# A decoder layer on one core: the experts' gates on the input rows, biases as contraction rows, a two-part second product summed in PSUM

## The reference

```python
scores = jnp.einsum('bsd,de->bse', x, Wr) + br
_, topk_idx = jax.lax.top_k(scores, K)
indicator = jax.nn.one_hot(topk_idx, E, dtype=scores.dtype).sum(-2)
weights = jax.nn.softmax(jnp.where(indicator > 0, scores, neg_inf), axis=-1)
for i in range(E):
    xi = x * indicator[..., i:i + 1]
    h = jax.nn.relu(jnp.einsum('bsd,dh->bsh', xi, W1[i]) + b1[i])
    yi = jnp.einsum('bsh,hd->bsd', h, W2[i]) + b2[i]
    out = out + yi * weights[..., i:i + 1]
```

## Time and profile before

| | |
|---|---|
| time, median of 3 runs | 346.68 us (345.67 to 348.85) |
| span of the profiled execution, first to last instruction | 345.2 us, 5907 instructions |
| median less the span | 1.5 us |
| VectorE busy | 205.2 us (59%) |
| ScalarE busy | 166.1 us (48%) |
| GpSimd busy | 56.2 us (16%) |
| mean granted TensorE clock | 0.975 of 2.4 GHz |
| cross attention of b = 3, its first score to the first `H` | 214.6 to 231.5 us |
| experts, first `H` to the end | 231.5 to 345.2 us |

### The profile page before, as it was taken

How to read it: one execution, slowest core, us unless ns; L and a number is a source line. 1 busy time by engine, 2 the same in 40 slices (tenths; PEclk the granted TensorE clock), 3 DMA queues, 4 the chain that set the end, 5 groups by cost and what they waited for, 6 DMA issues and landing times.

```text
span 345.2 us, 5907 instructions
## 1 busy us (share of the span) xinstructions
PE 311.9 (90%) x2177; PEld 233.1 (68%) x2194; DVE 205.2 (59%) x470; ACT 166.1 (48%) x482; POOL 56.2 (16%) x88
## 2 busy tenths in 40 slices
PE   6468999999998989797978888889999999999995
PEld 2356767787786667455634433458889998899895
DVE  3979766555639684974487886245455444433432
ACT  2435976747845664366445677844122112211310
POOL 5730047031003200740110201120020000000000
PEclk9859999999999999999989998999999999999999
DMA  7800002551100010001003680000000000100001
GB/s 220 202 1 1 2 2 38 65 63 18 41 6 3 4 46 0 0 5 47 2 5 66 237 235 3 2 0 2 0 2 1 3 0 2 30 2 0 2 0 30
DMA packets 13868, 11.98 MB, mean 35 GB/s; under 512 B 2600, under 2 KB 10896, under 8 KB 13840
## 3 DMA queue, kind: packets, MB, share of 16 engines
q1 hardware_dynamic: 13840, 11.61, 14.3%
HBM read 7.84 MB, written 0.52 MB: 24 GB/s over the span
## 4 chain that ended last, share of the span: by engine, by line
PE 74%; DVE 18%; issue 3%; ACT 3%; DMA 1%; another core or an unknown queue 0%; DVEq 0%; ACTq 0%
PE ps L775 17%; PE ps L514 7%; PE ps L515 7%; PE ps L516 7%; PE ps L587 6%; PE ps L620 4%; PE ps L632 4%; DVE mneg L1127 4%; PE ps L665 4%; PE ps L701 4%; PE ps L686 2%; PE ps L594 2%; PE ps L622 2%; DVE negmax L1096 2%; DVE norm L1010 2%
## 5 line engine op out<-in xcount | busy, mean ns | idle before, releaser
L891 ACT ACTIVATE p<-ps,negmax 128x256 f32<-128x256 f32 (+1 forms) x128 | 52.8, 431 | 25.5 <-DVE negmax L1096 25.2
L775 PEld LDWEIGHTS ps<-w_raw,hid 128*128 128x128 f32 x512 | 59.5, 192 | 1.4
L775 PE MATMUL ps<-w_raw,hid 128*128 128x128 f32 x512 | 59.6, 275 | 0.0
L943 ACT ACTIVATE hid<-ps,b1T 128x512 f32<-128x512 f32 x32 | 21.9, 688 | 73.8 <-PE ps L516 73.8
L1127 DVE TENSOR_REDUCE mneg<-ps 128x2 f32<-128x512 f32 x64 | 42.3, 684 | 14.3 <-PE ps L665 13.5
L920 ACT ACTIVATE px<-ps 128x512 f32<-128x512 f32 x64 | 35.4, 602 | 18.9 <-PE ps L686 15.9
L1219 DVE SCALAR_TENSOR_TENSOR resid<-ps,wgt,resid 128x128 f32<-128x128 f32 x64 | 18.0, 345 | 42.8 <-PE ps L775 42.8
L1096 DVE TENSOR_REDUCE negmax<-ps 128x2 f32<-128x512 f32 (+1 forms) x48 | 32.9, 686 | 17.3 <-PE ps L589 11.0
L665 PE MATMUL ps<-k_st,q_mem 128*128 128x256 bf16 x128 | 24.9, 278 | 8.9 <-DVE mneg L1127 8.1
L1200 DVE TENSOR_SCALAR hid<-ps,b1T 128x512 f32<-128x512 f32 x32 | 23.8, 749 | 10.9 <-PE ps L516 10.8
L877 ACT CAST t_hi<-ps 128x512 fp32r<-128x512 f32 x32 | 18.7, 594 | 20.9 <-PE ps L516 20.4
(11 more groups left out here) (175 smaller groups left out, 555.8 us busy)
## 6 DMA issues: line engine op xcount, KB each, us to landing
w_raw<-in_L_ffn_W SPq DMA_DIRECT2D x1, 2048.0 KB, 9.3
w_in<-in_L_attn_W_qkv SPq DMA_DIRECT2D x4, 384.0 KB, 5.2
k_st<-k_part SPq DMA_DIRECT2D x12, 128.0 KB
q_mem<-q_part SPq DMA_DIRECT2D x48, 32.0 KB
resid<-in_x SPq DMA_DIRECT2D x1, 512.0 KB, 4.6
p<-in_L_attn_W_o SPq DMA_DIRECT2D x1, 512.0 KB, 6.6
p<-in_ctx SPq DMA_DIRECT2D x1, 512.0 KB, 7.8
out_dram<-resid SPq DMA_DIRECT2D x2, 256.0 KB, 2.3
```

What stands on the lines that cost most here:

```text
L775: last = pe.matmul(ps[:, Y_BANK[k % 2], P * tt:P * tt + P], hid[:, k % 2, c, P * tt:P * tt + P], w2_sb[:, NC * e + c, :], start=(c == 0), ...
L891: last = act.activation(dst, bank[:, n * i:n * i + n], ACT.Exp, bias=negmax[:, kt, h:h + 1], accum_out=psums[:, kt, h:h + 1])
```

## The change

Four things change together.

First, the gate moves from the output to the input. Since relu is positively homogeneous and gates are not negative, gate x expert(x) equals the expert applied to gate x x, if the biases are scaled with it. A new unit `X` for each pass spreads the expert's gates over 128 partitions with one matmul (`gate_rows`), VectorE multiplies them with the transposed rows `nT` into `x_f` (`gated`), ScalarE makes the high part `x_hi` (`gated_high`), and VectorE the low part `x_lo` (`gated_low`). `H` of pass k waits for `x_lo` of pass k.

Second, biases enter by a contraction row. Normed rows sum to zero over their 128 columns, so the last column is dropped for a column of ones, the last row of W1 is subtracted from the other 127, and b1 takes its place. W1 is hence loaded as 127 rows, b1 as the 128th, and the dropped row is loaded once more, spread over all partitions (`w1_last`). GpSimd does the subtraction in eight steps (`first_weights`), and `WS` on ScalarE waits for these. The router's weights get the same treatment. The bias b2 is one float32 matmul for each half, in the pass with `B2`.

Third, the second product is two-part too. It has 12 matmuls of 128 x 512 columns, adds up in one PSUM bank over all eight experts of a half, and comes out transposed; at the end of a half `YE` copies it and `YO` transposes and adds it to `resid`. W2 is cut into parts by new units `W2` (ScalarE, in the slots of b = 3) and `second_weights` (GpSimd). For it, all four quarters of `hid` get a high part on ScalarE (`relu_high`) and a low part on VectorE (`relu_low`).

Fourth, `RT`, `GT` and `WT` of the first half move up into the slots of b = 3, and the five steps `oq0` to `wo` of the last batch element, which stood between `H` units of passes 0 to 3, stand together ahead of the first `H`.

```diff
+LAST = D - 1
+LOW = 32
...
+        px, w1_last, _, w2_hi, g_lo, t_hi, t_lo = overlay(
+            [("px", 4096, F32), ("w1_last", 4096, F32)], [("px_too", 4096, F32), ("w2_hi", 4096, F32R)],
+            [("g_lo", 2048, F32R), ("t_hi", 3072, F32R), ("t_lo", 3072, F32R)])
...
-            more = {(2, 1): [("b1", 0)], (3, 1): [("NT", 0)], (3, 7): [("RT", 0)]}
+            more = {(3, 1): [("NT", 0)], (3, 2): [("RT", 0)], (3, 4): [("GT", 0)], (3, 7): [("WT", 0)]}
...
-                if b == 2:
-                    slot += [("WS", 0, g)]
+                if b >= 2:
+                    slot += [("WS" if b == 2 else "W2", 0, g)]
...
+        slots.append([("X", 0), ("oq0", last), ("oT0", last), ("oq1", last), ("oT1", last), ("wo", last)])
+        extra = {3: [("NT", 1)], 4: [("RT", 1)], 5: [("GT", 1)], 6: [("WT", 1)], 9: [("YO", 0, 0), ("YO", 0, 1)]}
         for k in range(2 * NE):
-            more = extra.get(k, []) + [None, None]
-            units = [("H", k, 0), more[0], ("H", k, 1), ("H", k, 2), more[1], ("H", k, 3)]
-            slots.append([u for u in units if u] + ([("Y", k - 1)] if k else []))
-        slots.append([("Y", 2 * NE - 1)])
...
+            units = [("YE", 0, 0), ("YE", 0, 1)] if k == NE + 1 else []
+            units += [("H", k, 0), ("H", k, 1)] + ([("X", k + 1)] if k + 1 < 2 * NE else [])
+            units += [("H", k, 2)] + extra.get(k, []) + [("H", k, 3)]
+            if k % NE == 2:
+                units += [("B2", k // NE)]
+            slots.append(units + ([("Y", k - 1)] if k else []))
+        slots.append([("Y", 2 * NE - 1), ("YE", 1, 0), ("YE", 1, 1), ("YO", 1, 0), ("YO", 1, 1)])
...
-            sp.dma_start(w1_raw[:, :].rearrange("p (e n) -> p e n", n=HID), w1.rearrange("e p n -> p e n")
-                         ).then_inc(s_w12[0], 16)
+            sp.dma_start(w1_raw[0:LAST, :].rearrange("p (e n) -> p e n", n=HID),
+                         w1[:, 0:LAST, :].rearrange("e p n -> p e n")).then_inc(s_w12[0], 16)
+            sp.dma_start(w1_raw[LAST:D, :], b1.rearrange("e n -> (e n)").unsqueeze(0)).then_inc(s_w12[0], 16)
+            sp.dma_start(w1_last[:, :].rearrange("p (e n) -> p e n", n=HID), w1[:, LAST, :].partition_broadcast(P)
+                         ).then_inc(s_wlast, 16)
+            sp.wait_ge(s_zero, 1)
+            for r in (0, LOW):
+                sp.dma_start(b2_sb[r:r + NE, :], b2).then_inc(s_b2, 16)
             stack_m(2)
-            sp.dma_start(w2_sb, w2.rearrange("e (c p) d -> p (e c) d", p=P)).then_inc(s_w12[1], 16)
+            sp.dma_start(w2_raw[:, :].rearrange("p (n d) -> p n d", d=D), w2.rearrange("e (c p) d -> p (e c) d", p=P)).then_inc(s_w12[1], 16)
...
             for hf in range(2):
...
-                sp.wait_ge(s_acc, NE * (hf + 1))
-                sp.dma_start(out.rearrange(tiles, p=P)[:, 4 * hf:4 * hf + 4, :],
-                             resid[:, 4 * hf:4 * hf + 4, :]).then_inc(s_out, 16)
...
+                for i in range(2):
+                    ts = slice(4 * hf + 2 * i, 4 * hf + 2 * i + 2)
+                    sp.wait_ge(s_misc_ev, misc_at[("YO", hf, i)] + 1)
+                    sp.dma_start(out.rearrange(tiles, p=P)[:, ts, :], resid[:, ts, :]).then_inc(s_out, 16)
...
+                pool.wait_ge(s_mv3, TPB * (b + 1))
+                step(pool.memset(norm[:, TPB * b:TPB * b + TPB, LAST:D], 1.0))
+                norm_batch(2, b, s_mv3, s_n3, LAST)
+
+            def first_weights(i):
+                if i == 0:
+                    pool.wait_ge(s_w12[0], 32)
+                    pool.wait_ge(s_wlast, 16)
+                cols = slice(512 * i, 512 * i + 512)
+                pool.tensor_tensor(w1_raw[0:LAST, cols], w1_raw[0:LAST, cols], w1_last[0:LAST, cols], ALU.subtract
+                                   ).then_inc(s_wdiff, 1)
+
+            def second_weights(i):
+                pool.wait_ge(s_w2hi, i + 1)
+                cols = slice(512 * i, 512 * i + 512)
+                pool.tensor_tensor(w2_lo[:, cols], w2_raw[:, cols], w2_hi[:, cols].bitcast(F32), ALU.subtract
+                                   ).then_inc(s_w2lo, 1)
...
+            pool.wait_ge(s_misc, misc_at[("PJ", B - 1)] + 1)
+            pool.memset(b2_sb[:, :], 0.0).then_inc(s_zero, 1)
...
+            pool.tensor_tensor(wr_sb[0:LAST, :], wr_sb[0:LAST, :], wr_last[0:LAST, :], ALU.subtract).then_inc(s_pick, 1)
+            for i in range(NE):
+                first_weights(i)
             norm_3(0)
             norm_3(1)
             norm_3(2)
+            for i in range(4):
+                second_weights(i)
             norm_3(3)
+            for i in range(4, NE):
+                second_weights(i)
...
+            def gate_rows(k):
+
+                e, hf = k % NE, k // NE
+                if k == 0:
+                    pe.wait_ge(s_pv_ev, 2 * B)
+                if e == 0:
+                    pe.wait_ge(s_misc_ev, misc_at[("WT", hf)] + 1)
+                ge(pe, s_xf, k)
+                pe.matmul(ps[:, X_BANK, :], pick[:, e, :], wgtT[:, 512 * hf:512 * hf + 512], start=True, stop=True
+                          ).then_inc(s_gt, 1)
...
+                e = k % NE
                 if k == 0 and c == 0:
                     pe.wait_ge(s_wlo, 8)
                     pe.wait_ge(s_px, 16 * B)
                     pe.wait_ge(s_mx_ev, 16 * B)
-                if k % NE == 0 and c == 0:
-                    pe.wait_ge(s_misc_ev, misc_at[("NT", hf)] + 1)
+                if c == 0:
+                    pe.wait_ge(s_xlo, k + 1)
                 if k >= 1:
-                    pe.wait_ge(s_ha if c % 2 == 0 else s_hd, 2 * (k - 1) + c // 2 + 1)
-                products(ps[:, H_BANK[c], :], [w[:, e, P * c:P * c + P] for w in w1_p], n_of(512 * hf, 512)).then_inc(s_h, 1)
+                    pe.wait_ge(s_hd, 4 * (k - 1) + c + 1)
+                products(ps[:, H_BANK[c], :], [w[:, e, P * c:P * c + P] for w in w1_p],
+                         [x[:, k % 2, :] for x in x_p]).then_inc(s_h, 1)
...
-                for tt in range(4):
-                    for c in range(NC):
-                        last = pe.matmul(ps[:, Y_BANK[k % 2], P * tt:P * tt + P], hid[:, k % 2, c, P * tt:P * tt + P],
-                                         w2_sb[:, NC * e + c, :], start=(c == 0), stop=(c == NC - 1))
...
+                e, hf = k % NE, k // NE
+                out_bank = ps[:, Y_BANK[hf], :]
+                pe.wait_ge(s_w2lo, e + 1)
+                for c in range(NC):
+                    pe.wait_ge(s_hd, 4 * k + c + 1)
+                    w, h = [w[:, NC * e + c, :] for w in w2_p], [x[:, k % 2, c, :] for x in hid]
+                    pe.matmul(out_bank, w[0], h[0], start=(e == 0 and c == 0), stop=False)
+                    pe.matmul(out_bank, w[1], h[0], start=False, stop=False)
+                    last = pe.matmul(out_bank, w[0], h[1], start=False, stop=(e == NE - 1 and c == NC - 1))
                 last.then_inc(s_y, 1)
+
+            def second_bias(hf):
+                pe.wait_ge(s_b2, 32)
+                pe.matmul(ps[:, Y_BANK[hf], :], b2_sb[:, :], wgtT[:, 512 * hf:512 * hf + 512].bitcast(F32),
+                          start=False, stop=False)
...
             def weight_high(i):
 
-                act.wait_ge(s_w12[0], 16)
+                act.wait_ge(s_wdiff, i + 1)
                 act.copy(w1_hi[:, 512 * i:512 * i + 512], w1_raw[:, 512 * i:512 * i + 512]).then_inc(s_whi, 1)
 
-            def relu(k, c):
+            def second_high(i):
+
+                act.wait_ge(s_w12[1], 16)
+                act.wait_ge(s_wdiff, NE)
+                act.copy(w2_hi[:, 512 * i:512 * i + 512], w2_raw[:, 512 * i:512 * i + 512]).then_inc(s_w2hi, 1)
+
+            def gated_high(k):
+                act.wait_ge(s_xf, k + 1)
+                act.wait_ge(s_px, 16 * B)
+                ge(act, s_h, 4 * (k - 1))
+                act.copy(x_p[0][:, k % 2, :], x_f[:, k % 2, :]).then_inc(s_xhi, 1)
+
+            def relu_high(k, c):
                 act.wait_ge(s_h, 4 * k + c + 1)
                 ge(act, s_y, k - 1)
-                act.activation(hid[:, k % 2, c, :], ps[:, H_BANK[c], :], ACT.Relu,
-                               bias=b1T[:, NC * (k % NE) + c:NC * (k % NE) + c + 1]).then_inc(s_ha, 1)
...
+            def gated(k):
+                hf = k // NE
+                dve.wait_ge(s_gt, k + 1)
+                ge(dve, s_xhi, k - 1)
+                dve.tensor_tensor(x_f[:, k % 2, :], ps[:, X_BANK, :], nT[:, 512 * hf:512 * hf + 512], ALU.mult
+                                  ).then_inc(s_xf, 1)
+
+            def gated_low(k):
+                dve.wait_ge(s_xhi, k + 1)
+                dve.tensor_tensor(x_p[1][:, k % 2, :], x_f[:, k % 2, :], x_p[0][:, k % 2, :].bitcast(F32), ALU.subtract
+                                  ).then_inc(s_xlo, 1)
+
+            def relu_low(k, c):
+                dve.wait_ge(s_ha, 4 * k + c + 1)
+                dve.scalar_tensor_tensor(hid[1][:, k % 2, c, :], ps[:, H_BANK[c], :], 0.0,
```

(1 more changed line is left out.)

230 lines of the change are left out of this document (118 added, 112 removed).

## The result

The changed kernel takes 453.86 us (median; 449.52 to 456.13), against 346.85 us (345.67 to 348.85) measured beside it: 1.307 times the time before, 95% interval 1.301 to 1.312. It is 107 us slower. The forecast was 433.5 us in a range of 418 to 455. The profiled execution took 449.52 us, with a span of 447.7.

A forecast was written before the change was run, and what follows sets the result against it. TensorE was taken to bound the kernel, busy 90% of the span. Span 345.2 + 81 (stall) + 2.5 (cross attention) + 3.3 (experts with entry) = 432.0, median 1.5 above: 433.5 us, range 418 to 455.

The forecast's parts named there:

- The cause: W1's load: 127 outer rows, a prime, go through one DMA engine at 25.4 GB/s, taking 81.8 us; chance 0.84.
- Case (2): W1's load is spread over the engines anyway, with a remainder: time 358.5 us; chance 0.10.
- case (3): W1's load goes through one slow engine at 8 GB/s and takes 260 us: 611 us; chance 0.03.
- The stall: TensorE's first score of b = 2 waits for `stack_m(2)` behind W1, from 198.06 to 279.3: 81 us later.
- Cross attention: Cross attention of b = 3: eight W2 casts on ScalarE with earlier `RT` and `WT` add 2.5 us, between 0 and 5.
- After a stall of 80 us TensorE may be granted less than full clock for a while: Cross attention behind the stall waits for VectorE and ScalarE anyway, so a lower TensorE clock was put at nothing.
- So it costs nothing beyond the 81: GpSimd's eight W1 subtractions, 1.1 us each, are covered by the stall, since ScalarE wants one every 2 us.
- the earlier `RT` and `WT`: First-half routing steps moved into cross attention of b = 3, counted within its 2.5 us.
- The way into the experts: From the last `CO` to the first `H`: a chain of 7.7 us in which TensorE hardly works.
- A pass: Each expert pass takes 6.1 us, set by VectorE's and ScalarE's chain, against TensorE's own 5.8 and 6.37 before.
- small steps of `YE`: Experts: an odd piece within 4.5 us that also holds `RT` and `GT` of the second half and b2 products.
- the engine's rate: Rate of the one engine carrying W1, 407 / 16 GB/s; 10% lower or higher is 8 us to either side.

The follow-up runs named there:

- b_127_1: The kernel before with only W1's load cut into 127 rows and one row, nothing else of the change: 425.96 us, 1.226 times the kernel before.
- f_nolast: W1's correction and `w1_last` load left out, against the changed kernel with 112 and 15 row loads and `w1_last` behind `stack_m(2)` (374.84 us): 368.12 us.
- f_exp: Gates' exponential at `GT` instead of `RT`, against the changed kernel with 112 and 15 row loads and `w1_last` behind `stack_m(2)` (374.84 us): 370.82 us.
- a_m2_first: The changed kernel with `stack_m(2)` issued ahead of W1 on SyncE's queue: 459.47 us, against 453.86 us for the changed kernel.
- a_122_5: The changed kernel with W1's 127 rows loaded as 122 rows and 5 rows: 414.10 us, against 453.86 us for the changed kernel.

## Why the prediction was right, and where its terms were off

**The cause was right.** One engine carries the 127 rows: share 0.07, 26 GB/s (predicted 0.06 and 25), and cutting the load differently moves the time to where the number of engines says. Case (2), a split with a remainder, is out; of case (3), 8 GB/s, nothing is seen. That the wait for `stack_m(2)` and that for the weights have one cause and don't add was right too: with the first taken away, the second stands for 92 us.

**The stall was put at 81 us and took 83.7.** TensorE began at 281.73, where 279.3 was expected. `w_last` was issued at 262.06 and landed 17.9 us later by the page, at 280.0, where I had 278.8; the copies of `stack_m(2)` came 1.8 us behind it, where I had 0.5. What I had wrong without a price is the queue: I had taken these copies to be waiting in it long since, but SyncE was held at the bias row (74.76 us) and at the two copies of `b2` (8.60 us) and issued them only from 271.16 to 275.25. That is still ahead of the landing of `w_last`, so no row shows that it cost anything.

**Cross attention was put at +2.5 us (0 to 5) and took +9.9.** This is the term that was off most, at twice its upper bound. The starts of `CO` show where. Here are the first and the third `CO` of b = 3 in the changed kernel, then in `b_127_1`, which has the same pause and none of the rest:

```profile
306.60 1.07 PE L758 MATMUL ps<-px,v_pad 128*32 128x256 f32 x16
...
320.38 1.94 PE L758 MATMUL ps<-px,v_pad 128*32 128x256 f32 x16
```

```profile
298.15 1.07 PE L702 MATMUL ps<-px,v_pad 128*32 128x256 f32 x16
...
306.04 1.07 PE L702 MATMUL ps<-px,v_pad 128*32 128x256 f32 x16
```

From the first score of b = 2 to the first of these it is 24.9 us in the changed kernel, 23.6 in `b_127_1` and 21.3 in the kernel before. So 2.3 us come with the pause ("After a stall of 80 us TensorE may be granted less than full clock for a while ... I put nothing for it"), and 1.3 with what the change adds to b = 2. There I had of GpSimd's eight subtractions "So it costs nothing beyond the 81". They took 1.33 us each where I expected 1.1. What was missed is VectorE, whose low parts of W1 beside them took 1.25 and 1.79 us in place of 0.68, and TensorE waits for maxima behind them (0.42, 1.17 and 0.54 us). The 4.0 us of `f_nolast` are not this price, since `w_last` came late there.

From the first to the third `CO` of b = 3 it is 13.8 us against 7.9, both in `b_127_1` and before: 5.9 us, the largest part. It is "the earlier `RT` and `WT`", with `GT`, which I had within the 2.5. `f_exp` brings the same stretch from 13.6 to 10.1, so in that base 3.5 us hang on the place of one exponential in ScalarE's order and on the clock behind it. W2's casts, the only part that I did count, stand here too; with six of them gone the stretch took 12.3, and the whole cross attention 0.7 less. The last 0.4 us lie behind the third `CO`. The shares of 2.3 and 1.3 come from one profiled execution each, and the clock dips at other places in each of them, so they are good to some tenths at best.

On VectorE beside GpSimd the rows come first: operations that read one input from PSUM didn't change (all 64 `hid_lo` 0.68 to 0.69, two maxima 1.28), and those with both in SBUF went from 0.68 to 1.79 at most; one `x_lo` beside GpSimd's work on W2, at 340.83, took only 0.73. The Trainium skill, "SBUF — State Buffer", section "SBUF: two separate sides", states that a VectorE operation with two SBUF inputs and a GpSimd operation that reads SBUF shut each other out for a whole instruction. This trace agrees in which operations suffer.

**The way into the experts was put at 7.7 us and took 9.1.** The chain was right; `x_lo` took 1.60 us in place of 0.68, beside GpSimd's low parts of W2, and TensorE's own pieces ran partly at half clock (0.78 on average).

**A pass was put at 6.1 us and took 6.15.** The chain of VectorE and ScalarE holds it, not TensorE's 5.8: at 416.56, as in other passes, TensorE's first weight load of a pass stands 0.52 us for `x_lo`. That load, and three starts of `x_f` in the changed kernel:

```profile
416.56 0.19 PEld L571 LDWEIGHTS ps<-x_hi,w_hi 128*128 128x128 f32 x1 [0.52 <-DVE x_lo L1301]
...
390.48 0.68 DVE L1296 TENSOR_TENSOR x_f<-ps,nT 128x512 f32<-128x512 f32 x1
...
396.64 0.68 DVE L1296 TENSOR_TENSOR x_f<-ps,nT 128x512 f32<-128x512 f32 x1
...
406.75 0.68 DVE L1296 TENSOR_TENSOR x_f<-ps,nT 128x512 f32<-128x512 f32 x1
```

6.16 us, and then 10.11. That last one isn't in my sum: "small steps of `YE`" had a copy in mind, not that both pairs of turned tiles use bank 7, so that TensorE stands 3.66 us for VectorE's addition, in the middle of a pass. From the first `H` to the end I expected 109.3 us and it took 113.5; this wait is 4.0 of the 4.2.

**From span to median.** The span was put at 432.0 and is 447.7: +2.7 stall (with rounding), +7.4 cross attention, +1.4 entry, +4.2 experts. The median lies 6.2 us above that span, not 1.5, since the profiled execution was the fastest of four, with the highest mean granted clock (0.869, the others 0.850 to 0.860), and this kernel's times lie 6.6 us apart where those before lie 3.2 apart. That the median lies within the range is in part luck: the room was left for the engine's rate, which was nearly right, and terms without a price took it up. Each term was within 8 us, but nearly all were off to the same side, and that brought the time to the top of the range. The main term was priced from rows and held; the small ones were priced alone, as if nothing ran beside them.

## What to carry to other kernels

Before cutting one row off a tile, look at what is left for the outer dimension of its load: here 127 rows cost 79 us by themselves (`b_127_1`), and 122 rows 34 more than 112 and 15 in two loads. Follow such a load not only to its own user but to what is queued behind it, on the issuing queue and on each engine that handles it in order, because taking away one of several waits on one load gives nothing. And where small steps are moved between engines' chains, price them with their neighbours: in these runs a step that another engine stood for in the middle of a pass cost its whole wait (3.66 us), and mostly the clock behind it (2.7 us more).

## What the runs showed of the hardware that was not expected

- A transfer behind a slow one can hold the engine that issues it. SyncE stood 74.76 us (74.87 in `b_127_1`, 74.14 in `a_m2_first`) at the transfer behind the 127 rows, and 33.69 us at the two loads of `a_122_5`. Everything after it in SyncE's order was not even issued until then. In the changed kernel the hold ended at 262.02, before the load can have landed (2.08 MB at 26 GB/s from 186.80 on take until 266.8, an estimate), so it isn't the landing that ends it; what does, perhaps room in a queue, no run here shows.
- The granted clock is 0.5 in a pause of 77 us of TensorE, and the 36 us behind it took 2.3 us more than without the pause (0.88 against 0.95). Behind a pause of 3.66 us it fell in eight profiled executions and not in a ninth; where it did, a pass took 11.36 to 12.77 us in place of 10.11.
- One low part of [128, 512] on VectorE with both inputs in SBUF takes 0.68 us alone and up to 1.79 us beside GpSimd's subtraction, which itself took 1.33 us on average.
